# Slot attention on one core: gate scaling and row weights moved from ScalarE and TensorE operands to VectorE

## The chip, the core and the metric

The kernel runs on one core of a Trainium2 chip. One launch computes a stack of eight layers on 16 sequences of 128 tokens with 128 features. The metric is the device time of a launch in microseconds. A core has five engines that run their own instruction streams and wait for each other through semaphores: TensorE (PE in the profile, PEld for its weight loads), VectorE (DVE), ScalarE (ACT), GpSimd (POOL) and SyncE (SP), which here issues most of the DMAs.

## The reference, cut to what matters

The layers alternate between a cross-attention-like part and a feed-forward part, each on the layernorm of x, each added to x with a gate. The change touches the seventh (the code's layer 6), a slot attention with a GRU cell, three iterations:

```python
def rmsnorm(x, w, eps=EPS):
    return x * jax.lax.rsqrt(jnp.mean(x * x, axis=-1, keepdims=True) + eps) * w

def gru_cell(x, h, wi, wh, bi, bh):
    gi = jnp.einsum('...d,ed->...e', x, wi) + bi
    gh = jnp.einsum('...d,ed->...e', h, wh) + bh
    ...
    r = jax.nn.sigmoid(ir + hr)
    z = jax.nn.sigmoid(iz + hz)
    n = jnp.tanh(inn + r * hn)
    return (1.0 - z) * n + z * h

Pn = rmsnorm(P, input_norm_w)
k_proj, v_proj = Pn @ Wk.T, Pn @ Wv.T          # shapes (b, m, d), shortened here
for _ in range(NUM_ITERS):                      # 3
    q = rmsnorm(slots, slot_norm_w) @ Wq.T
    scores = jnp.einsum('bkd,bmd->bkm', q, k_proj) * scale
    attn = jax.nn.softmax(scores, axis=-2)
    attn = attn / (jnp.sum(attn, axis=-1, keepdims=True) + EPS)
    updates = jnp.einsum('bkm,bmd->bkd', attn, v_proj)
    slots = gru_cell(updates, slots, gru_wi, gru_wh, gru_bi, gru_bh)
```

The first softmax is over the slots k; the second scaling divides by the sum over the inputs m.

## The kernel before

All 2048 tokens are kept as columns of [128, 2048] tiles, in four chunks of 512 columns (four sequences, BC = 4). `cs(c)` is a chunk, `tok(b)` the 128 columns of a sequence. `nT` holds the slots, `buf[0..3]` and `share[0..1]` are work tiles, `bank(n)` are the eight PSUM banks.

Layer 6 runs in seven half-iterations, "halves" 0 to 6. A half does the attention of two chunks ("attend", a0 and a1) and the cell of the two chunks whose attention the half before made ("cell", c0 and c1). Half 0 has no cell and half 6 no attention. Each engine walks the same halves in its own program order; order is otherwise kept by the semaphores `X6[...]`.

Attention of a chunk: PE makes the scores with the slots (L2296) and the mean of squares (L2303); ACT makes 1/rms from it by Ln (L2376) and Exp (L2377); VectorE multiplies (L2433) and takes the least value (L2434); ACT takes the exponents in place in `buf[1]`, one sequence at a time with the row sum at its side (L2393); VectorE takes the reciprocals `rc` of the four row sums (L2463). Here a partition is an input m, so a row sum runs over the slots. The sum over the inputs is one over partitions, and PE makes it (L2327): for each sequence the weights loaded are the column `rc` repeated 128 times, the moving data are the exponents. ACT makes its inverse by Ln and Exp (L2365, L2366). VectorE then forms exponent x `rc` x inverse in `buf[2]`, a sequence at a time (L2426).

Cell of a chunk: PE sums the recurrent product (L2312) and the update product (L2337) for the two gates; ACT takes tanh of half of each (L2383, L2384), since sigmoid(v) = 0.5 tanh(v/2) + 0.5; an Identity activation turns the first into the reset gate (L2385) and another, in halves 1 to 4, makes 1 - z from the second (L2400). PE makes the candidate products (L2337, L2321), VectorE puts the candidate together (L2467 for the kept part, L2476, L2477), ACT takes its tanh (L2402), and VectorE mixes the new slots (L2458, L2459). In halves 5 and 6 VectorE does 1 - z itself with the layer's gate folded in (L2469) and adds to `xT` (L2471, L2451, L2452). PE waits in the order c0, c1, a0, a1 in the second part of a half, then makes L2332 (the recurrent candidate product for the next half) and goes on to the next half's scores. L2379 and L2407 are ACT's two loads of activation tables in a half. Half 6's PE work stands apart in `pe_last_cell` (L2345, L2337, L2353). L1930 and L1938 prepare folded weights during half 0.

VectorE's order in a half: a square (L2421), shares of c0 and c1, scores of a0 and a1, kept and candidate of c0, kept of c1, weights of a0 (`dve_weights6`), candidate of c1, weights of a1, the new slots. `link(ins)` makes an engine wait for its own instruction's result.

Of the kernel before, what the change touches and what calls it, by code (L numbers as in the profile page):

```python
# [5 lines left out]
B, S, D = 16, 128, 128  # L6
# [34 lines left out]
def flamingo_kernel(nc, ins, out, stop=LAYERS):  # L41
# [5 lines left out]
    with ExitStack() as ctx:  # L47
# [45 lines left out]
        def bank(n, w=512):  # L93
            return ps[:, 512 * n:512 * n + w]
# [33 lines left out]
        def tok(b):  # L128
            return slice(b * S, (b + 1) * S)
# [2154 lines left out]
        def pe_layer6(te):  # L2284
            for half, (attend, cell) in enumerate(halves()):
                if half == 1:
                    te.wait_ge(F7["thr"], 2)
                    te.wait_ge(X6["side"], VG_0 + len(VG_UNITS))
                for it, c in attend:
                    if it:  # L2290
                        te.wait_ge(X6["slots"], NCH * (it - 1) + c + 1)
                    else:
                        te.wait_ge(s_norm, NCH * 4 + min(c + 2, NCH))
                    for t in range(BC):
                        b = c * BC + t
                        mm = te.matmul(bank(4 + c)[:, t * S:(t + 1) * S], kq[:, tok(b)], nT[:, tok(b)], start=True, stop=True)  # L2296
                    mm.then_inc(X6["s_ps"], 1)
                    if half == 0 and c == 1:
                        te.wait_ge(F7["thr"], 1)
                        te.wait_ge(s_rstd, NCH * 4 + 3)  # L2300
                        te.matmul(bank(7)[:, 0:2], ones[:], thr[:, 0:2], start=True, stop=True).then_inc(F7["sum"], 1)
                    te.wait_ge(X6["sq" if c % 2 == 0 else "sq_dve"], 2 * it + c // 2 + 1)
                    te.matmul(bank(c), mean_w, buf[0][:, cs(c)], start=True, stop=True).then_inc(X6["var"], 1)  # L2303
                if half == 0:
                    te.wait_ge(s_norm, NCH * 5)
                    pe_update_w(te, 4, len(VG_UNITS))
                if half == 2 * ITERS:
                    pe_last_cell(te)
                    continue
                for it, c in cell:  # L2310
                    te.wait_ge(X6["rinv"], NCH * it + c + 1)
                    te.matmul(bank(c), gru_w[:, 3 * D:4 * D], nT[:, cs(c)], start=True, stop=False)  # L2312
                    te.wait_ge(X6["share"], NCH * it + c + 1)
                    for j in range(2):
                        mm = pe_update(te, j, c, bank(4 * j + c), False)
                    mm.then_inc(X6["rz_ps"], 1)
                for j in range(2):
                    for it, c in cell[j:j + 1]:
                        te.wait_ge(X6["rz"], NCH * it + c + 1)
                        pe_update(te, 2, c, bank(c), True)  # L2320
                        te.matmul(bank(4 + c), gru_w[:, 5 * D:6 * D], nT[:, cs(c)], start=True, stop=True).then_inc(X6["g_ps"], 1)  # L2321
                for j in range(2):
                    for it, c in attend[j:j + 1]:
                        te.wait_ge(X6["attn"], NCH * it + c + 1)
                        for t in range(BC):
                            b = c * BC + t
                            mm = te.matmul(bank(c)[:, t * S:(t + 1) * S], rc[:, c, t:t + 1].to_broadcast([128, 128]), buf[1][:, tok(b)],  # L2327
                                           start=True, stop=True)
                        mm.then_inc(X6["sum_ps"], 1)
                if half < 2 * ITERS - 1:  # L2330
                    for it, c in attend:
                        te.matmul(bank(4 + c), gru_w[:, 4 * D:5 * D], nT[:, cs(c)], start=True, stop=False)  # L2332
# [27 lines left out]
        def act_layer6(act, link):  # L2360
            for half, (attend, cell) in enumerate(halves()):
                for j in range(2):
                    for it, c in cell[j:j + 1]:
                        act.wait_ge(X6["sum_ps"], NCH * it + c + 1)
                        link(act.activation(buf[0][:, cs(c)], bank(c), ACT.Ln, bias=eps6[:]))  # L2365
                        act.activation(buf[0][:, cs(c)], buf[0][:, cs(c)], ACT.Exp, scale=-1.0).then_inc(X6["rinv"], 1)  # L2366
                    if j == 0:
                        for it, c in attend[0:1]:
                            if it:
                                act.wait_ge(X6["slots"], NCH * (it - 1) + c + 1)  # L2370
                            else:
                                act.wait_ge(s_norm, NCH * 4 + c + 1)
                            act.activation(buf[0][:, cs(c)], nT[:, cs(c)], ACT.Square).then_inc(X6["sq"], 1)
                for it, c in attend:
                    act.wait_ge(X6["var"], NCH * it + c + 1)
                    link(act.activation(buf[0][:, cs(c)], bank(c), ACT.Ln, bias=eps6[:]))  # L2376
                    act.activation(buf[0][:, cs(c)], buf[0][:, cs(c)], ACT.Exp, scale=-0.5).then_inc(X6["rstd"], 1)  # L2377
                if cell:
                    act.preload_act_table_set("exp_and_others")  # L2379
                for it, c in cell:  # L2380
                    act.wait_ge(X6["rz_ps"], NCH * it + c + 1)
                    at = c - 2 if half == 2 * ITERS else c
                    act.activation(buf[0][:, cs(c)], bank(at), ACT.Tanh, scale=0.5, bias=lnw6[:, 0:1])  # L2383
                    link(act.activation(buf[1][:, cs(c)], bank(4 + at), ACT.Tanh, scale=0.5, bias=lnw6[:, 1:2]))  # L2384
                    act.activation(buf[0][:, cs(c)], buf[0][:, cs(c)], ACT.Identity, scale=0.5, bias=half6).then_inc(X6["rz"], 1)  # L2385
                for j in range(2):
                    if half == 0:
                        act_update_w(act, 4 + 2 * j, 6 + 2 * j)
                    for it, c in attend[j:j + 1]:
                        act.wait_ge(X6["ein"], NCH * it + c + 1)  # L2390
                        for t in range(BC):
                            b = c * BC + t
                            ins_ = act.activation(buf[1][:, tok(b)], buf[1][:, tok(b)], ACT.Exp, scale=-1.0, bias=least[:, j, t:t + 1],  # L2393
                                                  accum_out=total[:, j, t:t + 1])
                        ins_.then_inc(X6["e"], 1)
                if half == 0:
                    act_update_w(act, 8, len(VG_UNITS))
                for it, c in cell:
                    if half < 2 * ITERS - 1:
                        act.activation(share[0][:, cs(c)], buf[1][:, cs(c)], ACT.Identity, scale=-0.5, bias=half6)  # L2400
                    act.wait_ge(X6["t"], NCH * it + c + 1)
                    act.activation(buf[3][:, cs(c)], buf[3][:, cs(c)], ACT.Tanh, bias=col("gru_bi", 2)).then_inc(X6["n"], 1)  # L2402
                if half == 2 * ITERS:
                    act_square(act, 7, 0, bank(0))
                    act_square(act, 7, 1, bank(1))
                if cell:
                    act.preload_act_table_set(LN_EXP)  # L2407

        def dve_layer6(dve, link):
            for half, (attend, cell) in enumerate(halves()):  # L2410
# [10 lines left out]
                    dve.tensor_tensor(buf[0][:, cs(c)], nT[:, cs(c)], nT[:, cs(c)], MUL).then_inc(X6["sq_dve"], 1)  # L2421
                for it, c in cell:
                    dve.wait_ge(X6["rinv"], NCH * it + c + 1)
                    for t in range(BC):
                        b = c * BC + t
                        ins_ = dve.scalar_tensor_tensor(buf[2][:, tok(b)], buf[1][:, tok(b)], rc[:, c, t:t + 1], buf[0][:, tok(b)], MUL, MUL)  # L2426
                    ins_.then_inc(X6["share"], 1)
                for j, (it, c) in enumerate(attend):

                    eb = buf[1][:, cs(c)].rearrange("p (b k) -> p b k", b=BC)  # L2430
# [29 lines left out]

        def dve_weights6(dve, link, it, c):
            dve.wait_ge(X6["e"], NCH * it + c + 1)
            dve.reciprocal(rc[:, c, :], total[:, c % 2, :]).then_inc(X6["attn"], 1)  # L2463

        def dve_kept6(dve, link, half, it, c):
            dve.wait_ge(X6["rz"], NCH * it + c + 1)
            kept = dve.scalar_tensor_tensor(share[1][:, cs(c)], buf[1][:, cs(c)], 1.0, nT[:, cs(c)], ADD, MUL)  # L2467
            if half >= 2 * ITERS - 1:
                dve.tensor_scalar(share[0][:, cs(c)], buf[1][:, cs(c)], minus_g6, half_g6, MUL, ADD)  # L2469
                link(kept)  # L2470
                link(dve.scalar_tensor_tensor(xT[:, cs(c)], share[1][:, cs(c)], half_g6, xT[:, cs(c)], MUL, ADD))  # L2471

        def dve_cand6(dve, link, it, c):
            bt = buf[3][:, cs(c)]
# [277 lines left out]
```

## Time and profile before

| | us |
|---|---|
| median of 3 runs | 757.95 (753.97 to 758.37) |
| the profiled execution | 758.14 |
| its span in the profile | 756.3 |
| PE busy in the span | 655.7 (87%) |
| VectorE busy | 572.8 (76%) |
| ScalarE busy | 525.6 (70%) |
| GpSimd busy | 319.4 (42%) |
| mean granted clock of TensorE | 0.947 |

The rows further down are from this one execution; times are microseconds from the span's start. A busy share is an average over stages. The slot layer fills about 596 to 724 us of the span.

### The profile page before, as it was taken

Reading aid. Unit: us, or ns where it says so; the run is one execution under the profiler, and the core shown is the slowest. Engines: PE = TensorE matmul, PEld = TensorE weight load, DVE = VectorE, ACT = ScalarE, POOL = GpSimd, SP = SyncE. Lnnn points to the kernel's source line nnn. Section 1 sums busy time; section 2 is a strip of 40 time slices with the busy share of each in tenths; the row PEclk is TensorE's granted clock in tenths of the full one; section 3 lists DMA queues with packets and bytes.
Section 4 is the critical chain, followed back from the end, with each engine's and each line's share of the span. In section 5 each row is a group of like instructions: output and inputs, shape, how many; then the busy total and the mean of one; then the engine's idle time right before and its main releaser. Section 6 shows DMA issues by size and latency. Waiting matters only on the chain.

```text
span 756.3 us, 13768 instructions
## 1 busy us (share of the span) xinstructions
PE 655.7 (87%) x5031; PEld 451.2 (60%) x5039; DVE 572.8 (76%) x1105; ACT 525.6 (70%) x1074; POOL 319.4 (42%) x337
## 2 busy tenths in 40 slices
PE   6288999488997998998799999988999998888967
PEld 5167887233554554655795666546888686666622
DVE  5869997887898857998565888668973346666777
ACT  4775663567885764677438776747885689999877
POOL 4776675787766778881000000189930040000000
PEclk8579999799999999999799999989999999999998
DMA  8526482111110114410000000700000000000001
GB/s 301 173 57 181 130 136 70 49 45 35 38 38 25 33 51 76 66 38 12 1 1 1 0 1 1 281 2 1 2 1 1 1 1 1 1 0 1 1 0 55
DMA packets 40273, 36.11 MB, mean 48 GB/s; under 512 B 21800, under 2 KB 30256, under 8 KB 40208
## 3 DMA queue, kind: packets, MB, share of 16 engines
q1 hardware_dynamic: 33616, 21.73, 9.8%
q0 software_dynamic: 6592, 13.51, 7.6%
q8 instruction: 41, 0.67, 0.4%
q14 instruction: 24, 0.20, 0.1%
HBM read 30.11 MB, written 5.11 MB: 47 GB/s over the span
## 4 chain that ended last, share of the span: by engine, by line
PE 57%; DVE 19%; ACT 13%; issue 4%; DMA 3%; POOL 3%; SPq 0%; ACTq 0%; DVEq 0%; POOLq 0%
PE ps L1351 5%; PE ps L1567 4%; PE ps L1604 3%; PE ps L2073 3%; PE ps L1002 3%; PE ps L2337 3%; PE ps L2024 3%; PE ps L1595 3%; PE ps L213 2%; ACT big L2393 2%; PE ps L1585 2%; POOL pe L400 2%; PE ps L217 2%; PE ps L1031 2%; PE ps L1516 2%
## 5 line engine op out<-in xcount | busy, mean ns | idle before, releaser
L1497 POOL DMA_INDIRECT pe<-in_rpe,idx x128 | 135.0, 1055 | 35.7 <-issue 24.5
L1963 POOL TENSOR_SCALAR big<-big,wcols 128x256 f32<-128x256 f32 x1 | 0.9, 937 | 138.9 <-DMA big<-in_l3f_w 138.9
L384 POOL DMA_INDIRECT pe<-normed_rows,pe x46 | 48.6, 1057 | 20.2 <-issue 10.1
L525 ACT ACTIVATE pe<-ps,wcols 128x256 f32<-128x256 f32 x92 | 38.5, 476 | 22.4 <-PE ps L432 22.4
L1707 ACT ACTIVATE big<-ps,small 128x128 f32<-128x128 f32 x128 | 34.7, 382 | 17.5 <-PE ps L1595 17.5
L1212 ACT ACTIVATE big<-ps 128x1024 f32<-128x1024 f32 x32 | 32.6, 1019 | 18.1 <-PE ps L999 17.9
L1351 PE MATMUL ps<-nT,big 128*128 128x512 f16 x192 | 44.5, 379 | 0.0
L432 PE MATMUL ps<-big 128*128 128x256 f16 x276 | 36.8, 287 | 5.6 <-DVE big L578 4.4
L2337 PEld LDWEIGHTS ps<-big,pe 128*128 128x128 f32 x288 | 34.3, 192 | 11.9 <-ACT big L2385 5.9
L1232 DVE TENSOR_REDUCE small<-ps 128x16 f32<-128x1024 f32 x32 | 38.3, 1216 | 1.5 <-PE ps L993 1.5
L2337 PE MATMUL ps<-big,pe 128*128 128x128 f32 x288 | 35.5, 277 | 1.8 <-ACT big L2385 1.8
L400 POOL DMA_INDIRECT pe<-tile_results,pe x32 | 30.6, 955 | 14.7 <-issue 7.3
L1567 PE MATMUL ps<-big,pe 128*128 128x128 f32 x256 | 32.2, 291 | 4.1 <-DVE big L1412 3.8
L1002 PE MATMUL ps<-big 32*128 32x512 f16 x192 | 26.9, 384 | 9.5 <-DVE xT L1275 8.1
L2235 DVE TENSOR_TENSOR big<-small,big 128x528 f16<-128x528 f32 x32 | 30.4, 974 | 5.6 <-ACT big L2105 5.4
L432 PEld LDWEIGHTS ps<-big 128*128 x276 | 27.7, 102 | 11.3 <-issue 7.3
L1567 PEld LDWEIGHTS ps<-big,pe 128*128 128x128 f32 x256 | 31.7, 207 | 4.3 <-issue 3.9
L665 DVE TENSOR_TENSOR big<-pe,big 128x512 f16<-128x512 f32 x46 | 32.5, 705 | 1.6
L1383 ACT ACTIVATE big<-ps,wcols 128x1024 f32<-128x1024 f32 x16 | 17.8, 1115 | 22.2 <-PE ps L1351 22.2
L1604 PEld LDWEIGHTS ps<-vx,big 128*128 128x128 f32 x256 | 31.1, 192 | 2.7 <-issue 0.5
L1351 PEld LDWEIGHTS ps<-nT,big 128*128 128x128 f16 x192 | 18.8, 98 | 21.8 <-issue 3.4
L1604 PE MATMUL ps<-vx,big 128*128 128x17 f32 x256 | 29.7, 258 | 0.0
(429 smaller groups left out, 1971.2 us busy)
## 6 DMA issues: line engine op xcount, KB each, us to landing
pe<-in_l2f_w SPq DMA_DIRECT2D x16, 256.0 KB, 6.1
tile_results<-big SPq DMA_DIRECT2D x23, 128.0 KB, 2.2
pe<-in_xrow SPq DMA_DIRECT2D x4, 512.0 KB, 5.3
big<-in_l0x_w SPq DMA_DIRECT2D x8, 256.0 KB, 7.0
pe<-in_rpe,idx POOLq DMA_INDIRECT x128
cT<-in_cT SPq DMA_DIRECT2D x2, 512.0 KB, 4.6
nT<-in_l0x_w SPq DMA_DIRECT2D x4, 256.0 KB, 7.7
vx<-in_l0x_w SPq DMA_DIRECT2D x4, 256.0 KB
```

The lines of the kernel that those rows point to most:

```text
L384: pool.indirect_dma_start(out=xg16[:, i % RX, h, :, :].rearrange("p r n -> p (r n)"), out_offset=None, in_=xrows_d, in_offset=bass.Indirec ...
L400: pool.indirect_dma_start(out=y2[:, b, j, :], out_offset=None, in_=y_d, in_offset=bass.IndirectOffsetOnAxis(ap=place[:, at:at + 1], axis=0 ...
L432: mm = te.matmul(hidden_ps(i, u)[:, f % 2, :], w_flat[:, bass.ds(at + (2 * F * a + f * 128), 128)], xt16[:, i % RT, b, :], start=(n == 0), ...
L525: ins_ = act.activation(hid32[:, i % RF, f, :], hidden_ps(i, u)[:, f % 2, :], ACT.Relu, bias=wcols[:, bass.ds(at + (COL_AT["l0x_b1"][0] + ...
L1002: return te.matmul(bank(4 + t % 2), kT[quad(t), p, tok(b)], qblk1[quad(t), b % QS, r, :, :], start=(part == 0), stop=False)
L1232: dve.tensor_reduce(mxp[:, b % 2, 2 * u:2 * u + 2, 0:8], ps[:, 1024 * u:1024 * (u + 1)].rearrange("p (t g k) -> p t g k", t=2, k=BLK), AX, ...
L1351: mm = te.matmul(bank(at + r), w3[:, a, w * D:(w + 1) * D], qT[:, 2 * (k // NC) + r, b, :], start=(i == 0), stop=(i == 2))
L1497: pool.indirect_dma_start(out=pe[:, v * D:(v + 1) * D], out_offset=None, in_=ins["rpe"], in_offset=bass.IndirectOffsetOnAxis(ap=idx[:, v:v ...
L1567: mm = te.matmul(bank(1 + f % 3)[:, j * 128:(j + 1) * 128], peT[:, f * VG + j, :], qblk[:, :, f * VG + j, :], start=True, stop=True)
L1604: mm = te.matmul(bank(6 + b % 2)[:, h * HW2:(h + 1) * HW2], dx[:, b % 2, h, :], vx4[:, b, h, :], start=True, stop=True)
L1707: ins_ = act.activation(dx[:, st % 2, h, :], bank(4 + j)[:, (h % 4) * S:(h % 4 + 1) * S], ACT.Exp, bias=a4[:, g:g + 1])
L2337: mm = te.matmul(dst[:, t * S:(t + 1) * S], vg[g][:, tok(b)], buf[2][:, tok(b)], start=start, stop=start or t == BC - 1)
```

## The change

Three edits, all in layer 6. (1) ACT's two Identity activations go; `X6["rz"]` is signalled by the second tanh, and VectorE makes 0.5 t + 0.5 in `buf[0]` and, in halves 1 to 4, 0.5 - 0.5 t in `share[0]`, both in `dve_kept6`. (2) `dve_weights6` multiplies the exponents of the chunk in place with the reciprocals, after them, before it signals `X6["attn"]`; the share is then one product of a chunk without `rc`. (3) The column sums of a chunk are one product with a tile of ones.

```diff
@@ pe_layer6
-                        for t in range(BC):
-                            b = c * BC + t
-                            mm = te.matmul(bank(c)[:, t * S:(t + 1) * S], rc[:, c, t:t + 1].to_broadcast([128, 128]), buf[1][:, tok(b)],
-                                           start=True, stop=True)
-                        mm.then_inc(X6["sum_ps"], 1)
+                        te.matmul(bank(c), ones[:], buf[1][:, cs(c)], start=True, stop=True).then_inc(X6["sum_ps"], 1)
@@ act_layer6
-                    link(act.activation(buf[1][:, cs(c)], bank(4 + at), ACT.Tanh, scale=0.5, bias=lnw6[:, 1:2]))
-                    act.activation(buf[0][:, cs(c)], buf[0][:, cs(c)], ACT.Identity, scale=0.5, bias=half6).then_inc(X6["rz"], 1)
+                    act.activation(buf[1][:, cs(c)], bank(4 + at), ACT.Tanh, scale=0.5, bias=lnw6[:, 1:2]).then_inc(X6["rz"], 1)
...
-                    if half < 2 * ITERS - 1:
-                        act.activation(share[0][:, cs(c)], buf[1][:, cs(c)], ACT.Identity, scale=-0.5, bias=half6)
@@ dve_layer6
-                    for t in range(BC):
-                        b = c * BC + t
-                        ins_ = dve.scalar_tensor_tensor(buf[2][:, tok(b)], buf[1][:, tok(b)], rc[:, c, t:t + 1], buf[0][:, tok(b)], MUL, MUL)
-                    ins_.then_inc(X6["share"], 1)
+                    dve.tensor_tensor(buf[2][:, cs(c)], buf[1][:, cs(c)], buf[0][:, cs(c)], MUL).then_inc(X6["share"], 1)
@@ dve_weights6
-            dve.reciprocal(rc[:, c, :], total[:, c % 2, :]).then_inc(X6["attn"], 1)
+            link(dve.reciprocal(rc[:, c, :], total[:, c % 2, :]))
+            eb = buf[1][:, cs(c)].rearrange("p (b k) -> p b k", b=BC)
+            dve.tensor_tensor(eb, eb, rc[:, c, :].unsqueeze(2).to_broadcast([128, BC, S]), MUL).then_inc(X6["attn"], 1)
@@ dve_kept6
+            else:
+                dve.tensor_scalar(share[0][:, cs(c)], buf[1][:, cs(c)], -0.5, 0.5, MUL, ADD)
+            link(dve.tensor_scalar(buf[0][:, cs(c)], buf[0][:, cs(c)], 0.5, 0.5, MUL, ADD))
```

## Rows read from the trace of the kernel before

**Rows 1.** Busy time by stage: stretch, length, each engine's busy us, PE clock, DMA.
```profile
632.80:651.80 19.00, 16.76 (x99) 11.98 (x98) 12.77 (x26) 17.74 (x38) 0.00 (x0) 1.00 0.00 1
689.80:709.00 19.20, 16.10 (x94) 11.43 (x94) 14.86 (x30) 17.03 (x36) 0.00 (x0) 1.00 0.00 0
```

**Rows 2.** Chain that ended last, half 2: start, us, engine, tile, line.
```profile
634.77 1.12 PE ps L2303 x2
...
641.15 1.80 PE ps L2337 x16
...
644.27 0.72 ACT big L2385
644.99 3.08 ACT big L2393 x16
648.07 0.61 ACT pe L2400
...
650.53 1.28 ACT L2407
...
653.75 1.12 PE ps L2303 x2
```

**Rows 3.** Timeline of half 2: start, us, engine, line, operation, tiles, count, idle before.
```profile
643.66 1.02 PE L2321 MATMUL ps<-nT,big 128*128 128x512 f32 x2
...
644.73 0.75 DVE L2476 SCALAR_TENSOR_TENSOR big<-ps,wcols,big 128x512 f32<-128x512 f32 x1 [1.64 <-PE ps L2321]
...
646.72 0.17 DVE L2463 RECIPROCAL small<-small 128x4 f32<-128x4 f32 x1
...
647.89 0.69 DVE L2477 TENSOR_TENSOR big<-ps,big 128x512 f32<-128x512 f32 x1
...
648.49 0.17 DVE L2463 RECIPROCAL small<-small 128x4 f32<-128x4 f32 x1
...
648.72 1.16 PE L2327 MATMUL ps<-big,small 128*128 128x128 f32 x8 [0.62 <-DVE small L2463]
...
649.71 1.88 PE L2332 MATMUL ps<-nT,big 128*128 128x512 f32 x4
...
651.43 1.05 PE L2296 MATMUL ps<-nT,l1f_w 128*128 128x128 f32 x8
```

**Rows 4.** Groups by line and shape, VectorE: busy us, mean ns, idle before.
```profile
L2426 DVE SCALAR_TENSOR_TENSOR big<-big,small 128x128 f32<-128x128 f32 x48 | 14.8, 372 | 7.8 <-ACT big L2366 7.7
...
L2421 DVE TENSOR_TENSOR big<-nT 128x512 f32<-128x512 f32 x6 | 4.1, 689 | 0.1
...
L2469 DVE TENSOR_SCALAR pe<-big,small 128x512 f32<-128x512 f32 x4 | 2.2, 540 | 0.0
...
L235 DVE CAST vx<-nT 128x512 f16<-128x512 f32 x4 | 1.7, 426 | 0.1
```

**Rows 5.** Timeline of halves 5 and 6.
```profile
701.74 0.75 DVE L2476 SCALAR_TENSOR_TENSOR big<-ps,wcols,big 128x512 f32<-128x512 f32 x1 [0.59 <-PE ps L2321]
...
706.64 1.16 PE L2327 MATMUL ps<-big,small 128*128 128x128 f32 x8 [0.29 <-DVE small L2463]
...
707.63 3.60 PE L2345 MATMUL ps<-nT,big 128*128 128x512 f32 x8
...
711.14 4.73 PE L2337 MATMUL ps<-big,pe 128*128 128x128 f32 x40
...
721.87 0.72 ACT L2402 ACTIVATE big<-big,wcols 128x512 f32<-128x512 f32 x1 [2.51 <-DVE big L2477]
```

**Rows 6.** TensorE elsewhere: its timeline before 515.4, and two stretches with their clock.
```profile
508.51 3.80 PE L2148 MATMUL ps<-big,vx 128*128 128x264 f32 x16 [1.44 <-DVE big L2164]
514.24 2.72 PE L2148 MATMUL ps<-big,vx 128*128 128x264 f32 x8 [1.93 <-DVE big L2170]
...
495.00:501.70 6.70, 5.93 (x9) 0.50 0.00 0
515.50:518.80 3.30, 3.30 (x13) 0.50 0.02 5
```

## Prediction

> **What bounds the kernel now.** I read the table by stages first, to see how much room each engine has in the slot layer (596 to 724 us). The layer is seven half-iterations ("halves") numbered 0 to 6, and halves 2, 3 and 4 repeat with a period of 18.98 us: the first variance product starts at 634.77 and at 653.75 [rows 2]. In one half the stages show ACT busy 17.74 of 19.00 us, PE 16.76, DVE 12.77 [rows 1]. So ACT has almost no room and VectorE looks as if it had 6 us. This share is where a quick reading would stop; the question is who is waited for, and where VectorE's free time lies.
>
> The chain of waits of one half (half 2) answers the first part. It runs through PE from 634.77 to 642.95 (variance, scores, gate products), then changes to ACT for the rest: two tanh, the Identity of L2385 (0.72), sixteen pieces of L2393 (3.08), L2400, L2402, L2400, L2402 (0.61 each) and the table load of L2407, then Ln, Exp, Square, and back to PE at 653.75 [rows 2]. Of what is removed, one L2385 (0.72) and two L2400 (2 x 0.61) lie on it: 1.94 us a half.
>
> The timeline gives the second part. VectorE's stretch begins when PE has made the candidate product of the half's first cell chunk (c0): from 644.73 it does L2476, L2477, L2467, one reciprocal, L2476, L2477 and the second reciprocal at 648.49, nearly without a gap [rows 3]. PE's column sums (L2327) wait for those reciprocals. PE then does L2332 and the scores (L2296, from 651.43), is through by 651.43 + 0.89 = 652.32 and waits 1.43 us for ACT's Square. That 1.43 us is all the slack this route has.
>
> **The change, part by part.** Durations are of one operation; with no wait behind it the next VectorE operation starts about 0.08 before the end (0.61 after a tensor_tensor of 0.69), with a link 0.03 after the end.
>
> *ACT.* L2385 and L2400 go: 12 x 0.722 and 8 x 0.705 us of work. In time on its chain: 1.94 a half, if nothing else arrives later.
>
> *Shares (L2426).* Eight of 0.345 to 0.37 with starts 0.28 apart become two tensor_tensor of 0.69 [rows 4]: 1.14 becomes 0.69 a chunk. PE wants the product only after the recurrent gate product, well behind it, so in halves 1 to 5 this gains nothing; in half 6 it is covered by L2345 as well.
>
> *Column sums.* Eight narrow passes of L2327, 0.99 us from the first to the start of what follows (648.72 to 649.71), become two passes of 512 columns, which from standstill take about as long (L2303, 1.12 to its end, against 1.16 for L2327) [rows 2, 3]. Worth nothing.
>
> *VectorE's new work.* A whole half gets two linear steps per chunk, and one 128x512 product of exponents with the reciprocals per chunk. The product is like L2421, 0.69, since only an operand is broadcast. For the linear steps with constants there is no row: L2469, the same operation with two scalars read from memory, is 0.54, and the cast L235, the lightest one-source operation of that size, 0.43 [rows 4]. I take 0.43 (0.36 to the next start), and 0.54 as the upper end; a lower end of 0.30 would need it to beat the cast.
>
> The Trainium skill ("VectorE: DVE Perf Modes", the perf-mode tier table) lets an fp32 tensor_scalar run at double rate, but not a tensor_tensor; with that page's fixed term I get an estimate of 0.42 us. The sum by it is the one I make with 0.43; by the row of L2469 each half would come out 0.22 longer.
>
> *The chain.* Now VectorE's order from 644.73, with the new durations: L2476 0.78, L2477 0.61, L2467 of c1 0.61 (to 646.73), its two linear steps 0.36 + 0.46 (647.55), reciprocal 0.20, product 0.61 (first weights ready 648.44, before 646.89), L2476 of c1 0.78, L2477 0.61 (its result at 649.83, before 648.58), reciprocal 0.20, product 0.69: the second weights are ready at 650.64. Before it was 648.66. The second column sum therefore starts at 650.69 instead of 648.72, 1.97 us later [rows 3]. PE follows with 0.99 + 1.72 + 0.89 and reaches the variance product at 654.29 instead of waiting for it at 653.75. That is 0.54 late, but PE then arrives running and saves 0.26 of the start (1.12 became 0.86): **+0.28 us a half**. Everything after (scores, gates) hangs on PE as before. Queued behind the new work are the slots' last steps (L2458, L2459): c1's end 1.2 us later, but PE wants them 1 us after that.
>
> And ACT? It finishes the exponents 0.75 us earlier, has no L2400, and then waits for L2477 of c1 at 649.83: its last tanh starts at 649.88, the table load at 650.60 instead of 650.53 [rows 2]. The 1.94 us have turned into a wait for VectorE. Halves 1 to 4 hand this on four times: 4 x 0.28 = 1.1. With 0.54 for the steps it is 4 x 0.50 = 2.0; with 0.30, about 0.
>
> *Half 5* also has VectorE's L2469 and L2471 per chunk, and no ACT time to hide in. From 701.74: 0.78, 0.61, 0.61, L2469 0.46, L2471 0.77, linear step 0.46, reciprocal 0.20, product 0.61, 0.78, 0.61, 0.20, 0.69 = 6.78, so 708.52. Its column sum started at 706.64 and would start at 708.57, +1.93; L2345 (3.44) follows directly and before was only 0.07 short of being waited for [rows 5]: **+1.9**. *Half 6:* L2385 off brings the first step 0.7 forward, two linear steps of 0.46 and the wait for L2353 eat it up: VectorE's last result for ACT's L2402 (721.87) comes 0.2 later. Half 0's products lie under PE's L1930.
>
> Sum without clock effects: 1.1 + 1.9 + 0.2 = 3.2, on the profiled execution's 758.14 us (span 756.3): **761.3**. The median of the runs is 757.95, so nothing has to be corrected.
>
> **The clock.** This is what I think decides. In these halves PE now waits at most some 1.4 us at a time [rows 3], and its granted clock is 1.00 (the 2.4 GHz level) [rows 1]. Elsewhere it fell: 1.44 us idle, 3.80 us of work, 1.93 us idle, and at 515.4 the clock goes to 0.50 (1.2 GHz) for 3.4 us, though PE had just begun to work; in another place it stayed at 0.50 for 6.8 us [rows 6]. In the new half PE ends the last candidate product at about 646.25 (643.66 + 0.85 + 0.89 + 0.85, as the Identity in front of c1's is gone), waits 2.2 us for the first weights, sums for 0.9, waits 1.3 more, and only then has a long run. That is more idle time than in front of 515.4. In half 5 the two waits would be 2.8 and 1.5. A fall strikes just as PE starts the stretch that sets the pace. It costs half the slow time that PE works: 1.7 for 3.4 us, 3.4 for 6.8. As part of it falls into the wait, I take 2.4. Five halves offer it; with starting points unlike each other I reckon with three: 7.2.
>
> **768.5 us** is the forecast.
>
> The Trainium skill ("TensorE: Matmul & The Clock Gate", the table "Why this matters for your kernels") warns only of single idle gaps longer than any of mine. By its rule there would be no fall here and the time would be the rival's below, 761.3; the trace speaks against it with the 1.93 us gap before 515.4.
>
> **The rivals.**
> - *The chain without the clock.* VectorE ends last as worked out, the clock holds or falls once: 761.3, up to 764. For it: 1.00 throughout the layer now. Against it: the row at 515.4.
> - *ACT's relief arrives (faster).* If VectorE's stretch after 644.73 ended in time, 4 x 1.94 and 0.7 each from halves 5 and 6 would be saved, some 9 us: 749. It decides at VectorE: c1's L2477 would have to be done by about 647.9, where ACT would then stand, and the second weights by about 648.2 (651.81, the earlier start of the variance product, less PE's 3.6); my sum has 649.83 and 650.64. For it: VectorE's busy share. Against it: those 6 us of free time lie before 644.73, where nothing of the new work can be done.
> - *No change.* The linear steps are cheaper than the cast and half 5 absorbs some: 756 to 759.
>
> **How the numbers follow.** Clock falls two or more times: 0.55, 764 to 776 (two falls 766, five 773, plus the dearer linear steps). Chain alone: 0.32, 759 to 764. No change: 0.07. Relief: 0.06. The range 759 to 776 leaves out the last two and a little above. About 1% is what a measurement can tell, so "same" is 750.4 to 765.5: it takes the chain alone, no change and a sliver of the others: 0.38. Slower 0.57, faster 0.05.
>
> **What would show it.** In the new profile: the wait of the sums (L2327's place) for VectorE's product, 1.9 us or more, and of ACT's L2402 for L2477; no wait of PE's variance product for ACT's Square in halves 2 to 5; period 19.2 to 19.3 where the clock is 1.00, 21 to 22 where it fell; granted clock under 1.00 in the stage 632 to 709. VectorE busy some 15 us a half. I am wrong if the linear steps take under 0.3 us, if the period falls under 18.9, or, in the size, if the clock stays at 1.00 there.

## The result, and the profile after

| us | before | changed |
|---|---|---|
| median | 757.68 (6 runs, 753.97 to 758.37) | 771.37 (6 runs, 770.57 to 772.48) |
| ratio | 1 | 1.0183, 95% interval 1.0163 to 1.0203 |
| profiled execution | 758.14 | 770.75 |
| its span | 756.3 | 768.8 |
| mean granted clock | 0.947 | 0.932 |

The change costs 13.7 us. The 12.5 us between the two spans can be placed by the first variance product (L2303) of each half, which has the same line number in both kernels, and by the last tanh of the layer (721.87 before [rows 5], 734.22 after):

| stretch | before | changed | difference |
|---|---|---|---|
| up to half 0's product | 600.42 | 598.98 | -1.44 |
| half 0 | 15.47 | 15.40 | -0.07 |
| half 1 | 18.88 | 20.98 | +2.10 |
| half 2 | 18.98 | 22.42 | +3.44 |
| half 3 | 18.98 | 19.45 | +0.47 |
| half 4 | 18.98 | 21.98 | +3.00 |
| halves 5 and 6, to the start of the last tanh | 30.16 | 35.01 | +4.85 |
| the rest | 34.43 | 34.58 | +0.15 |

So it is all in the slot layer (13.79 us there, less the 1.44 us that this execution was faster ahead of it, where the code is the same), and within it there are two amounts: half 3 shows the smaller alone, halves 1, 2, 4 and 5 have something on top. The table by stages of the changed kernel separates them (stretch, length, then each engine's busy us with its count in the order PE, PEld, DVE, ACT, POOL, then the granted clock, DMA share, GB/s):

```profile
635.36:657.78 22.42, 19.24 (x86) 12.09 (x85) 14.40 (x25) 15.18 (x33) 0.00 (x0) 0.85 0.00 1
657.78:677.23 19.45, 16.27 (x87) 10.78 (x86) 13.36 (x24) 14.47 (x32) 0.00 (x0) 1.00 0.00 1
677.23:699.21 21.98, 19.27 (x86) 11.71 (x85) 15.45 (x27) 15.88 (x35) 0.00 (x0) 0.84 0.00 0
```

These are halves 2, 3 and 4. In the mean of the three, ACT's load fell from 17.74 [rows 1] to 15.2 us and VectorE's rose from 12.77 to 14.4 (a single half can differ by 1 us, because some operations slip over its edge), and no engine is full. Half 3 at clock 1.00 is 0.47 longer than before all the same. The busy shares explain nothing here; an order of waits does. Halves 2 and 4 differ from it by the clock: 0.85 and 0.84.

Half 3 in the timeline (start, us, engine, line, operation, tiles, count, idle before and releaser):

```profile
667.72 0.75 DVE L2471 SCALAR_TENSOR_TENSOR big<-ps,wcols,big 128x512 f32<-128x512 f32 x1 [1.80 <-PE ps L2321]
...
669.11 0.68 DVE L2459 SCALAR_TENSOR_TENSOR pe<-big,nT 128x512 f32<-128x512 f32 x1
...
669.71 0.42 DVE L2465 TENSOR_SCALAR pe<-big 128x512 f32<-128x512 f32 x1
...
670.04 0.42 DVE L2466 TENSOR_SCALAR big<-big 128x512 f32<-128x512 f32 x1
...
670.71 0.69 DVE L2455 TENSOR_TENSOR big<-big,small 128x512 f32<-128x512 f32 x1
671.32 0.75 DVE L2471 SCALAR_TENSOR_TENSOR big<-ps,wcols,big 128x512 f32<-128x512 f32 x1
671.46 1.13 PE L2325 MATMUL ps<-big,ones 128*128 128x512 f32 x2 [2.11 <-DVE big L2455]
...
672.83 0.72 ACT L2395 ACTIVATE big<-big,wcols 128x512 f32<-128x512 f32 x1 [2.00 <-DVE big L2472]
672.91 0.69 DVE L2455 TENSOR_TENSOR big<-big,small 128x512 f32<-128x512 f32 x1
...
673.66 1.12 PE L2325 MATMUL ps<-big,ones 128*128 128x512 f32 x2 [1.07 <-DVE big L2455]
```

This is the counterpart of [rows 3] (L2471 here is L2476 there, L2459 is L2467, L2325 is L2327, L2395 is L2402). VectorE starts on c0's candidate at 667.72 and runs without a gap until its second weights end at 673.60. PE waits for it twice (2.11 and 1.07), and ACT once (2.00): the time that left ACT has become that wait. The chain of waits, which in [rows 2] went from PE to ACT, now goes from PE to VectorE:

```profile
666.74 0.88 PE ps L2321 x2
...
667.72 0.76 DVE big L2471
...
671.40 0.67 DVE big L2471
672.10 0.69 DVE big L2472
672.79 0.10 DVE small L2453
672.91 0.70 DVE big L2455
673.66 1.12 PE ps L2325 x2
674.78 1.72 PE ps L2328 x4
676.50 0.89 PE ps L2296 x8
677.39 0.86 PE ps L2303 x2
```

No ACT line stands between the products of L2303 and the next half's; before, eight or more did.

The clock of TensorE in the layer (stretch, length, PE busy with its count, granted clock, DMA share, GB/s):

```profile
630.00:633.30 3.30, 3.05 (x4) 0.50 0.00 0
633.40:650.30 16.90, 14.66 (x81) 1.00 0.00 1
650.50:657.10 6.60, 5.87 (x9) 0.50 0.00 0
657.30:691.30 34.00, 28.71 (x159) 1.00 0.00 1
691.40:698.10 6.70, 6.09 (x8) 0.50 0.00 0
715.30:722.00 6.70, 6.01 (x7) 0.50 0.00 0
```

Four times it is at 0.50 (1.2 GHz), in halves 1, 2, 4 and 5. Each time it falls in the first column sum or in the wait behind it, 0.3 to 1.7 us before the second sum, and stays low into the run that everything waits for. Before, the layer was at 1.00.

### The profile page after: what moved, and what is told of

Read it like the earlier page. It is cut to its first block, busy times and chain, and to the rows that moved or that the text cites. A ratio compares the mean times of both kernels' runs of the same rounds, so it can differ in the third digit from the quotient of the medians.

```text
span 768.8 us, 13608 instructions
## 1 busy us (share of the span) xinstructions
PE 662.8 (86%) x4959; PEld 446.7 (58%) x4967; DVE 581.2 (76%) x1101; ACT 512.5 (67%) x1054; POOL 320.4 (42%) x337
## 4 chain that ended last, share of the span: by engine, by line
PE 59%; DVE 22%; ACT 6%; POOL 5%; issue 5%; DMA 3%; SPq 0%; ACTq 0%; DVEq 0%; POOLq 0%
PE ps L1351 5%; PE ps L1567 4%; PE ps L2333 3%; PE ps L1604 3%; POOL pe L400 3%; PE ps L2073 3%; PE ps L1002 3%; PE ps L2024 3%; PE ps L1595 2%; PE ps L213 2%; PE ps L1585 2%; PE ps L1031 2%; PE ps L217 2%; PE ps L1516 2%; PE ps L1015 2%
## 5 line engine op out<-in xcount | busy, mean ns | idle before, releaser
L384 POOL DMA_INDIRECT pe<-normed_rows,pe x46 | 49.4, 1073 | 19.3 <-issue 10.7
L1707 ACT ACTIVATE big<-ps,small 128x128 f32<-128x128 f32 x128 | 34.7, 382 | 17.5 <-PE ps L1595 17.5
L400 POOL DMA_INDIRECT pe<-tile_results,pe x32 | 30.7, 959 | 13.7 <-issue 7.3
L2325 PE MATMUL ps<-big,ones 128*128 128x512 f32 x24 | 17.4, 822 | 16.3 <-DVE big L2455 16.3
```

Of the source, the lines that this page charges most:

```text
L384: pool.indirect_dma_start(out=xg16[:, i % RX, h, :, :].rearrange("p r n -> p (r n)"), out_offset=None, in_=xrows_d, in_offset=bass.Indirec ...
L400: pool.indirect_dma_start(out=y2[:, b, j, :], out_offset=None, in_=y_d, in_offset=bass.IndirectOffsetOnAxis(ap=place[:, at:at + 1], axis=0 ...
L1707: ins_ = act.activation(dx[:, st % 2, h, :], bank(4 + j)[:, (h % 4) * S:(h % 4 + 1) * S], ACT.Exp, bias=a4[:, g:g + 1])
```

## The experiments

The kernels run here were compared with the kernel before on the same chip. On these chips it took 881.5 us (first four kernels) and 882.9 us (last four) instead of 758: all kernels alike reached the slot layer some 120 to 132 us later. The profile puts 6 to 12% of their chain down to "another core or an unknown queue", and the mean granted clock was 0.88 to 0.90 instead of 0.947. The slot layer itself ran there within 0.1 us as on the first chip (the changed kernel took 135.14 us there and 135.24 here), so I compare layers, from half 0's variance product to the last tanh; the ratio of whole runs has an interval of about 0.3% to 0.4% to either side. "Periods" are those of halves 1 to 4. Before, the layer is 721.87 - 600.42 = 121.45.

**Keeping TensorE at work while it waits.**

```diff
@@ pe_layer6, ahead of the wait for the weights, halves 1 to 5
+                        if half:
+                            te.wait_ge(X6["rstd"], NCH * it + c + 1)
+                            for _ in range((2, 1)[j]):
+                                te.matmul(bank(c), mean_w, consts[:, 0:512], start=True, stop=True)
                         te.wait_ge(X6["attn"], NCH * it + c + 1)
```

> The changed kernel, with TensorE kept at work while it waits for the weighted exponents: two products of constants into the bank of the coming column sum ahead of the first wait, one ahead of the second, in halves 1 to 5. They compute nothing that is used. Theory (idleness lowers the clock): the granted clock stays at 1.00 from 610 to 735 us and the four low stretches of the layer go, which cost 1.5 + 3.0 + 2.5 + 3.0 = 10 us; the time is 761 to 762 and the period of a half 19.4 to 19.5. Rival (the clock falls for another reason, or the added products hold up the sums): 771 or more, low stretches stay. In the waits of L2303 and in VectorE's order nothing should change under either.

Measured: layer 125.14 us, 10.10 shorter than the changed kernel's; periods 19.44 four times, halves 5 and 6 31.97; whole run 1.0046 of before (1.0018 to 1.0074), where the layer's 3.69 us are 1.0042. The table by stages and two products of L2303, half 2's and half 3's:

```profile
741.50:851.20 109.70, 103.98 (x504) 1.00 0.00 1
...
780.38 1.02 PE L2303 MATMUL ps<-big,consts 128*128 128x512 f32 x2
...
799.82 1.02 PE L2303 MATMUL ps<-big,consts 128*128 128x512 f32 x2
```

The clock is 1.00 from half 1 to the end of the layer, and the time that the low stretches had cost is back. What is left, 3.7 us, is the order of waits. This splits the loss in two: 3.7 us chain, 10.1 us clock. The rival, that the clock falls for another reason, is out.

**The first edit alone.**

```diff
@@ act_layer6
-                    act.activation(buf[0][:, cs(c)], buf[0][:, cs(c)], ACT.Identity, scale=0.5, bias=half6).then_inc(X6["rz"], 1)
...
-                        act.activation(share[0][:, cs(c)], buf[1][:, cs(c)], ACT.Identity, scale=-0.5, bias=half6)
@@ dve_kept6
+            else:
+                dve.tensor_scalar(share[0][:, cs(c)], buf[1][:, cs(c)], -0.5, 0.5, MUL, ADD)
+            link(dve.tensor_scalar(buf[0][:, cs(c)], buf[0][:, cs(c)], 0.5, 0.5, MUL, ADD))
```

> Only the first edit on the kernel before: the gates' linear steps go from ScalarE to VectorE; reciprocals, column sums and shares as before. Theory (each product of weights costs 0.7 on VectorE's stretch, and the stretch sets the pace only when both edits are in): c1's L2477 ends at +0.5 against before, ScalarE still ends the half last, the half is 0.6 shorter (18.3 to 18.4), half 5 0.5 longer: 755.5 to 757, clock 1.00 in the layer. Rival (the linear steps alone do the harm): period 19.2 or more and 760 or more.

Measured: periods 18.24, 18.34, 18.34, 19.76; layer 122.35; whole run 1.0006 (0.9975 to 1.0038). The first three periods are what was expected, 0.64 shorter than before, so the linear steps do no harm to the order of waits in halves 1 to 4. What I had not expected is the fourth period: the clock fell in half 4 and again in half 5 (826.4), and with these two falls the layer is 0.9 us longer than before.

```profile
804.12 1.16 PE L2327 MATMUL ps<-big,small 128*128 128x128 f32 x8 [1.37 <-DVE small L2460]
805.57 1.74 PE L2327 MATMUL ps<-big,small 128*128 128x128 f32 x8 [0.29 <-DVE small L2460]
...
806.00:809.40 3.40, 3.40 (x10) 0.50 0.00 0
```

The waits are 1.37 and 0.29, the same as in halves 1, 2 and 3 of this kernel, and there the clock stayed up. The expectation of 755.5 to 757 missed by this (1.0006 of 757.95 would be 758.4); the mechanism of the chain stood.

**The second and third edit alone.**

```diff
@@ dve_weights6, with the matching edits of L2327 and L2426
-            dve.reciprocal(rc[:, c, :], total[:, c % 2, :]).then_inc(X6["attn"], 1)
+            link(dve.reciprocal(rc[:, c, :], total[:, c % 2, :]))
+            eb = buf[1][:, cs(c)].rearrange("p (b k) -> p b k", b=BC)
+            dve.tensor_tensor(eb, eb, rc[:, c, :].unsqueeze(2).to_broadcast([128, BC, S]), MUL).then_inc(X6["attn"], 1)
```

> Only the second and third edit on the kernel before: exponents weighted on VectorE, one product with ones a chunk, shares without the reciprocals; the linear steps stay on ScalarE. Theory: the second column sum starts 1.15 us later in a half, which TensorE's slack of 1.4 us covers, so the period stays 18.98 to 19.1; half 5 has no slack and becomes 1.4 longer; there the clock may fall (waits of 1.9 and 1.4 us): 759.0 without, 761.5 with a fall. Rival (the weights alone do the harm): 765 or more.

Measured: periods 18.88, 18.98, 18.98, 18.98, exactly those of before; halves 5 and 6 1.28 longer; layer 122.67, clock 1.00. The weights alone are covered by TensorE's slack, as expected.

```profile
791.03 1.12 PE L2325 MATMUL ps<-big,ones 128*128 128x512 f32 x2 [0.61 <-DVE big L2458]
...
792.49 0.69 DVE L2458 TENSOR_TENSOR big<-big,small 128x512 f32<-128x512 f32 x1
...
793.23 1.12 PE L2325 MATMUL ps<-big,ones 128*128 128x512 f32 x2 [1.07 <-DVE big L2458]
...
797.12 1.12 PE L2303 MATMUL ps<-big,consts 128*128 128x512 f32 x2
...
830.32 1.13 PE L2325 MATMUL ps<-big,ones 128*128 128x512 f32 x2 [1.93 <-DVE big L2458]
832.52 1.12 PE L2325 MATMUL ps<-big,ones 128*128 128x512 f32 x2 [1.07 <-DVE big L2458]
```

The second sum waits for VectorE's product, and still the variance product behind it starts on time. The last two lines are half 5: after waits of 1.93 and 1.07 us the clock held, as it did after 0.61 and 1.07 in halves 1 to 4. The whole run was 1.006 (1.0024 to 1.0095), 2.1 to 8.4 us, more than the 759 to 761.5 expected, and the layer gives only 1.2 of it. The rest I can't place: the five of its eight executions with a mean granted clock of 0.881 to 0.883 took 887.6 to 890.0 us, the three with 0.891 to 0.893 took 881.1 to 884.3, and the one kept trace is of the latter.

Together these two say that in halves 1 to 4 the longer chain comes from neither edit alone: the linear steps shorten ACT's side of the half by 0.64, the weights use up TensorE's slack, and only both together make VectorE's stretch the longest way round. Alone, the two cost the layer 0.9 us (by two falls of the clock) and 1.2 us (in half 5). They also say that the wide column sum does not bring the falls: the kernel that has it kept its clock, the one with the old narrow sums did not.

**Only 1 - z to VectorE.**

```diff
@@ dve_kept6, for c0
+            elif c % 2 == 0:
+                dve.tensor_scalar(share[0][:, cs(c)], buf[1][:, cs(c)], -0.5, 0.5, MUL, ADD)
@@ dve_layer6, behind the second dve_weights6, for c1 in halves 1 to 4
+                            dve.tensor_scalar(share[0][:, cs(c1)], buf[1][:, cs(c1)], -0.5, 0.5, MUL, ADD)
```

> On the kernel before, only 1 - z (L2400) goes to VectorE: c0's with its kept part, in VectorE's idle stretch, c1's behind the second reciprocal, where VectorE waits for ScalarE. The reset gate stays on ScalarE. Theory: ScalarE ends a half last, and two of 0.61 leave its chain while nothing is added ahead of c1's candidate: each of halves 1 to 4 is 1.0 to 1.2 shorter, 753 to 754 (ratio 0.994), period 17.8 to 18.0. Rival (TensorE or VectorE ends right behind ScalarE): period 18.7 or more, 757.

Measured: periods 17.70, 17.80, 17.80, 17.80; layer 116.81, 4.64 shorter than before, clock 1.00; whole run 0.9972 (0.9944 to 1.0000); the layer's 4.64 us alone would be 0.9947.

```profile
772.62 1.36 ACT L2400 ACTIVATE big<-big,wcols 128x512 f32<-128x512 f32 x2
773.14 0.17 DVE L2464 RECIPROCAL small<-small 128x4 f32<-128x4 f32 x1
773.23 0.40 DVE L2448 TENSOR_SCALAR pe<-big 128x512 f32<-128x512 f32 x1
```

ACT's two tanh now follow each other, and VectorE's new step (0.40) stands behind the last reciprocal, in a gap. Two steps of 0.61 off ACT's chain give 1.18 a half. The same operation that lengthens the half in the changed kernel, where c1's stands ahead of its candidate, is part of a gain here.

**The changed kernel again.** Nothing edited.

> The changed kernel as it is, next to the others of this call. Theory: its ratio to the kernel before is again 1.017 to 1.019, with a period of 19.4 in the halves without a low stretch and 21 to 22.5 with one, four low stretches (three to five) in the layer. Rival (the low stretches came from that one execution): none or one, period 19.4 throughout, 761 or 1.005.

Measured: 1.0176 (1.0134 to 1.0217); periods 20.93, 22.40, 19.44, 21.97, layer 135.14; four low stretches, again in halves 1, 2, 4 and 5 and of the same lengths:

```profile
761.60:764.90 3.30, 3.01 (x4) 0.50 0.00 0
782.10:788.70 6.60, 5.87 (x9) 0.50 0.00 0
823.10:829.70 6.60, 6.03 (x8) 0.50 0.00 0
847.00:853.60 6.60, 6.05 (x7) 0.50 0.00 0
```

So the pattern is not that of one execution. Half 3 is spared in both, and the falls begin at nearly the same places, 15.6, 15.1, 14.2 and 16.1 us into their halves in the first execution and 15.5, 15.0, 14.2 and 16.1 in this one. They are not the same place from half to half.

**One product of constants instead of three.**

```diff
-                            for _ in range((2, 1)[j]):
+                            for _ in range((1, 0)[j]):
```

> The changed kernel with a single product of constants, ahead of the first wait of each half alone: the waits become 1.2 and 1.1 us where they were 2.1 and 1.1. The product computes nothing that is used. Theory (the sum of idle time around the wait decides, and where it lies): none to two low stretches in the layer instead of four, period 19.44 in all other halves, layer 10 to 5 us shorter than the changed one's. Rival (only the complete cover helps): four low stretches remain, layer as long as the changed one's.

Measured (one execution): periods 20.99, 19.50, 21.21, 19.50; layer 130.04, halfway between the full cover (125.14) and none (135.24). Three low stretches of 3.4 us in place of one of 3.4 and three of 6.8:

```profile
757.30:760.50 3.20, 2.94 (x4) 0.50 0.00 0
764.00:798.00 34.00, 29.24 (x153) 1.00 0.00 0
798.20:801.40 3.20, 3.20 (x4) 0.50 0.02 5
839.20:842.40 3.20, 2.72 (x4) 0.50 0.00 0
...
776.27 1.12 PE L2329 MATMUL ps<-big,ones 128*128 128x512 f32 x2 [1.25 <-DVE big L2459]
```

With waits of 1.25 and 1.16 us the clock falls in halves 1 and 3 and not in 2 and 4; in half 5, with 2.16 and 1.16, it falls too. Over the kernels with no, one and three unused products, the low time shrinks with PE's idle time around the wait, as the theory has it (my bound of two low stretches was one too few). Which half is struck does not follow from the waits, and between kernels their length does not decide alone: 1.93 and 1.07 held above, 1.37 and 0.29 did not.

**The fill, and one step moved on VectorE.** On the first experiment's kernel, c1's 1 - z goes behind the second weights.

```diff
@@ dve_kept6
-            else:
+            elif c % 2 == 0:
                 dve.tensor_scalar(share[0][:, cs(c)], buf[1][:, cs(c)], -0.5, 0.5, MUL, ADD)
@@ dve_layer6, behind the second dve_weights6, in halves 1 to 4
+                            dve.tensor_scalar(share[0][:, cs(c1)], buf[1][:, cs(c1)], -0.5, 0.5, MUL, ADD)
```

> The changed kernel with TensorE kept at work as in the first experiment (products of constants that are not used), and with VectorE's 1 - z of chunk c1 moved from ahead of the weights to behind them. Theory (VectorE's stretch from c0's candidate to the second weights sets the pace, operation for operation): the period falls by that step's 0.34, to 19.10, and nothing else moves; the layer is 1.4 us shorter than with the fill alone. Rival (TensorE or ScalarE sets it): period stays 19.44.

Measured: periods 19.10, 19.10, 19.11, 19.10; layer 123.79, 1.35 shorter; whole run 1.0029 (0.9999 to 1.0059).

```profile
776.11 1.02 PE L2303 MATMUL ps<-big,consts 128*128 128x512 f32 x2
...
795.22 1.02 PE L2303 MATMUL ps<-big,consts 128*128 128x512 f32 x2
```

One operation of 0.42, whose place in the order costs 0.34, is worth 0.34 of every period. VectorE's stretch sets the pace one for one.

**1 - z on VectorE, and TensorE at work into the last layer.** The fourth experiment's kernel with three unused products in `pe_last_cell`.

```diff
@@ pe_last_cell
+            for _ in range(3):
+                te.matmul(bank(4), mean_w, consts[:, 0:512], start=True, stop=True)
             pe_var(te, 7, 0, bank(4))
```

> The kernel before with 1 - z on VectorE, c1's behind the second reciprocal, and with three products of constants, not used, at the end of the slot layer's work on TensorE, where it waits 2.9 us for ScalarE's first squares of the last layer. Theory: period 17.8 again; the fall of the clock right after that wait (723.6 in the kernel before) goes and gives back 1.5 us: about 752, or 0.992 of the kernel before. Rival (the fall only comes a little later): 0.994 as without the products.

Measured: 0.9931 (0.9902 to 0.9959), with the layer at 116.81 as without the products. On this chip it is faster than both given kernels (875.7 us against 882.9 and 898.6). Its interval overlaps that of the fourth experiment, and 0.9947, the layer's 4.64 us alone, lies in both. What the three products add stays open: in this kernel's profile the last layer starts at clock 1.00, but so it does in the profile of the fourth experiment, which has no such products, and from the last tanh to the end the two take 34.5 and 34.7 us.

## Why the prediction was right

The forecast was 768.5 with a range of 759 to 776, slower with 0.57; the median is 771.37. The mechanism was right in both parts, VectorE's stretch and the clock; two sizes were off.

*VectorE's stretch.* 5.96 from c0's candidate to the start of the second sum, in the profile 667.72 to 673.66, 5.94. The linear steps with constants, for which [rows 4] had only bounds, took 0.42 (forecast 0.43), the product with the broadcast operand 0.69, the wide column sum 1.12. The Trainium skill ("VectorE: DVE Perf Modes", the perf-mode tier table) had led to an estimate of 0.42, and the trace agrees; L2461, with scalars from memory, is 0.54 as before. Half 5's stretch was forecast as 6.83 us and measured 6.84 (709.15 to 715.99).

*ACT's relief.* It was to turn into a wait for VectorE: 2.00 us in half 3 before L2395.

*What a half costs.* Forecast 0.28, measured 0.47 (half 3) and 0.46 with the fill. This term was mis-sized, and the step is "PE arrives running and saves 0.26 of the start". From the start of the variance product to c0's candidate on VectorE it was 644.73 - 634.77 = 9.96 before and 667.72 - 657.78 = 9.94 after. The sum counted with starts as the timeline prints them, and there a product that follows another starts before that one ends: L2303 at 677.23 in the timeline, at 677.39 in the chain. So 0.16 of the 0.26 between 1.12 and 0.86 was only a matter of where a row starts; 0.10 is left at the product's end (1.02 against 1.12) and 0.02 at c0's candidate. Without it the sum was 0.54. Measured, the half is 9.94 + 5.94 + 3.57 = 19.45, the last from the second sum to the next variance product. The period of 19.2 to 19.3 that was named as a sign therefore did not come; VectorE's 15 us a half were 14.4.

*Half 5 and 6.* Forecast +1.9 and +0.2; with the clock held up, 31.97 - 30.16 = +1.81. All chain terms together: forecast 3.2, measured 3.69. Halves 1 to 4 cost 1.9 instead of 1.1, halves 5 and 6 cost 1.8 instead of 2.1.

*The clock.* Forecast were three low stretches at 2.4 each, 7.2. There were four: 1.5, 3.0, 2.5 (periods less 19.45) and 3.0 (35.01 less 31.97), 10.1 in all, 2.5 each. The price was right, the number one short. In the profiled execution the clock cost 2.9 more than forecast and the chain 0.5 more, while the stretch ahead of the layer took back 1.4; its span lies 2.1 above the forecast one, the median 2.9 above the forecast. That it came so near was in part luck: the three was a reckoning, and nothing in the rows told how many of the five halves would be struck. The waits in front were forecast as 2.2 and 1.3, and are 2.11 and 1.07 (half 5: 2.8 and 1.5, and are 3.01 and 1.07). The fill shows that idle time is needed for the falls: with PE at work the clock does not fall. What picks the half stays open.

The Trainium skill ("TensorE: Matmul & The Clock Gate", the table "Why this matters for your kernels") warns of single gaps longer than the waits of halves 1 to 4; only half 5's first one, 3.01 us, comes up to the length it names. By that rule the clock would have held in halves 1, 2 and 4, which lost some 7 of the 10.1 us. The trace does not agree: in halves 2 and 4 the longest gap was 2.11 us, in the first edit alone 1.37, in the kernel with one unused product 1.25, and the clock fell.

*The rival on the other side*, ACT's relief of 9 us, decided where the text had put it, at VectorE's stretch. Half of it can be had: with only 1 - z moved, and to places in which VectorE has nothing to do, the layer is 4.6 us shorter.

## What to carry to other kernels

Ask of an operation that is moved to an engine with idle time where that idle time lies in the order; VectorE, busy 67% of a half before the change, became the bound here, because its free third came before the work could start. The place of an operation was worth more than its length: in the changed kernel the same 0.4 us step cost 0.34 a half ahead of the weights and nothing behind them. And waits of one or two microseconds on TensorE, harmless by themselves, can lower its clock for the run that follows: here that was nearly three quarters of the loss.

## What the runs showed of the hardware

TensorE's clock fell after waits as short as 1.37 and 0.29 us with 1 us of work between, in one half of the four that had these waits, and around 2.11 and 1.07 in three halves of four. It held after 0.61 and 1.07 in four halves and after 1.93 and 1.07 in one. Each low stretch in the layer lasted 3.4 or 6.8 us; in the changed kernel one cost 1.5 to 3.0. Unused products in the waits, 0.86 us each, kept it at 1.00 over 109.70 us. Which half is struck repeated exactly in a second execution on another chip (halves 1, 2, 4 and 5, not 3), which suggests something steady that the waits alone don't tell. Two executions are all that was compared, and no run here shows what it is.
